# Attention of a cross-attention and expert layer: transposed projections of 512 columns, sums of squares by a matmul, scores on four 32-row tiles

## The reference

```python
q = layernorm(x) @ Wq.T                      # 32 heads of 16
k, v = context @ Wk.T, context @ Wv.T        # split from one concatenated kv
q, k = rmsnorm(q), rmsnorm(k)                # t * rsqrt(mean(t*t over 16) + 1e-6), each head by itself
scores = einsum('bhnd,bhmd->bhnm', q, k) * 16 ** -0.5
out = einsum('bhnm,bhmd->bhnd', softmax(scores), v)
x = x + out
```

## Time and profile before

| | before |
|---|---|
| median of 3 runs | 1083.45 us |
| the profiled execution: span from first to last instruction | 1096.4 us |
| first score matmul starts | 42.3 us |
| last score matmul starts | 532.3 us |
| first instruction of the second block's VectorE work | 538.80 us |
| TensorE busy in the span | 1011.1 us, 92% |
| VectorE, ScalarE, GpSimd busy | 726.6, 475.6 and 287.0 us |

### The profile page before, as it was taken

The page is one execution under the profiler, slowest core; times in us unless marked ns, Lnnn a source line. Parts: engine busy times, 40 slices in busy tenths (PEclk is TensorE's granted clock), DMA queues, the critical chain, the costliest instruction groups (busy, mean ns, idle before and its releaser), DMA issues.

```text
span 1096.4 us, 20598 instructions
## 1 busy us (share of the span) xinstructions
PE 1011.1 (92%) x7368; PEld 791.9 (72%) x7369; DVE 726.6 (66%) x1686; ACT 475.6 (43%) x670; POOL 287.0 (26%) x194
## 2 busy tenths in 40 slices
PE   3699999998999989999699999999999999999776
PEld 3555556565555665555299899999999899999666
DVE  6677876756676675765456887547474774765378
ACT  2256556545666446656723324233333342432111
POOL 3434444432343433432100010110101010101552
PEclk9899999999999999999879999999999999999889
DMA  9430000010000100000131015424242433332564
GB/s 321 159 116 2 1 1 2 20 59 3 1 1 30 49 3 1 21 20 1 49 136 67 20 32 187 158 69 171 70 174 75 179 120 121 139 90 77 163 193 144
DMA packets 32636, 88.90 MB, mean 81 GB/s; under 512 B 5040, under 2 KB 6576, under 8 KB 29104
## 3 DMA queue, kind: packets, MB, share of 16 engines
q1 hardware_dynamic: 25680, 65.34, 16.3%
q0 software_dynamic: 6880, 22.55, 6.9%
HBM read 65.33 MB, written 22.54 MB: 80 GB/s over the span
## 4 chain that ended last, share of the span: by engine, by line
PE 44%; DVE 4%; another core or an unknown queue 2%; issue 1%; ACT 1%; DVEq 0%; ACTq 0%
PE u_ps L958 14%; PE y_ps L958 13%; PE z_ps L958 13%; PE xt_ps L971 2%; DVE x_sb L1391 1%; PE z_ps L952 1%; DVE g_sb L1332 0%; PE xt_ps L984 0%; DVE u_lo L1320 0%; DVE stats L1174 0%; DVE x_sb L1351 0%; DVE g_hi L1335 0%; ACT u_hi L1093 0%; DVE hot_row L1285 0%
## 5 line engine op out<-in xcount | busy, mean ns | idle before, releaser
L454 ACT ACTIVATE probs<-scores 128x1024 f32<-128x1024 f32 x256 | 247.8, 1030 | 164.7 <-PE scores L332 164.7
L204 POOL TENSOR_TENSOR rsqrt<-mean_sq,power 128x16 f32<-128x16 f32 (+1 forms) x69 | 193.0, 2798 | 312.2 <-DVE mean_sq L556 277.3
L958 PE MATMUL z_ps<-u_hi,w_sb 128*128 128x256 f32 x896 | 167.9, 285 | 2.0 <-DVE u_lo L1320 1.6
L958 PE MATMUL u_ps<-x_hi,w_sb 128*128 128x256 f32 x896 | 165.1, 282 | 4.4 <-issue 2.3
L958 PE MATMUL y_ps<-w_sb,g_hi 128*128 128x512 f32 x448 | 143.9, 402 | 12.6 <-DVE g_lo L1337 8.4
L1093 ACT ACTIVATE u_hi<-u_ps,b_ug 128x256 fp32r<-128x256 f32 x112 | 47.1, 472 | 237.0 <-PE u_ps L958 233.0
L958 PEld LDWEIGHTS u_ps<-x_hi,w_sb 128*128 128x128 f32 x896 | 140.4, 190 | 7.2 <-issue 3.8
L958 PEld LDWEIGHTS z_ps<-u_hi,w_sb 128*128 128x128 f32 x896 | 141.0, 190 | 2.9 <-DVE u_lo L1320 2.0
L344 PE MATMUL o_ps<-probs,v_sb 128*32 128x512 f32 x1024 | 136.4, 604 | 0.5 <-ACT probs L454 0.3
L958 PE MATMUL z_ps<-u_lo,w_sb 128*128 128x256 f32 x448 | 126.3, 282 | 0.1
L958 PE MATMUL u_ps<-x_lo,w_sb 128*128 128x256 f32 x448 | 125.9, 281 | 0.0
(11 more groups left out here) (149 smaller groups left out, 1774.4 us busy)
## 6 DMA issues: line engine op xcount, KB each, us to landing
w_raw<-w_all SPq DMA_DIRECT2D x27, 1024.0 KB, 6.9
y_dram<-y_sb SPq DMA_DIRECT2D x40, 256.0 KB, 2.1
ctx_sb<-ctx_t SPq DMA_DIRECT2D x4, 1024.0 KB, 7.3
out<-x_sb SPq DMA_DIRECT2D x16, 256.0 KB
y_dram<-zeros SPq DMA_DIRECT2D x1, 3584.0 KB, 23.6
x_sb<-x SPq DMA_DIRECT2D x1, 3072.0 KB, 20.1
xn_dram<-xn SPq DMA_DIRECT2D x12, 256.0 KB, 2.1
bd<-b_down SPq DMA_DIRECT2D x9, 256.0 KB, 3.4
```

Of the source, the lines that this page charges most:

```text
L204: nc.gpsimd.tensor_tensor(rsqrt[:, half, 0:width], mean_sq[:, half, 0:width], power[:, 0:width], ALU.pow).then_inc(rsqrt_ready, 1)
L454: nc.scalar.activation(probs[:, s % 2, 2 * a:2 * a + 2, :], scores[:, a], ACT.Exp, scale=float(HD) ** 0.5).then_inc(p_ready, 1)
L958: ins = nc.tensor.matmul(out_ps, stat[a], mov[b], start=(first and a + b == 0), stop=(last and a == 1), skip_group_check=True)
```

## The change

The attention's block is written anew, for all 16 units without a hardware loop. A unit is again a group of 8 heads with 8 steps.

- q and k are made **transposed**, head dimensions on partitions: 12 float32r matmuls of 512 columns each per group (`q_passes` in three parts of 4, `k_chunk` in four of 3). v is made for all 32 heads at a time, 12 matmuls per 128 context rows, 4 times per sequence (`v_all`). The normalized x has hi and lo now too.
- The **sums of squares** over 16 partitions come from ScalarE's square and one float32 matmul with a block matrix of ones (`sum_q`, `sum_k`). The inverse root is ScalarE's Ln and Exp and one Newton step, the latter on VectorE (`first_root_*`, `newton_*`).
- The **stack** of hi and lo is made by VectorE: a shuffle of the 32 lanes of each quadrant doubles 16 dimensions to 32, a cast makes hi, and one more instruction lo (`stack_q`, `stack_k`). A contraction is now over 32 rows, with k_hi and k_lo in two rounds: **8 score matmuls on four tiles of 32 rows**, into all four banks of `scores`.
- ScalarE takes **one exponential of 2048 columns** per step, and the next scores wait for it (`p_ready`, t).
- Two banks (`bank_a`, `bank_b`) take k, q and v, and one (`tr`) everything else.
- x, context and weights arrive in a layout that a DMA reads in one piece per partition; context and weights are loaded in another order, and the first expert's weights later.

The core of the diff, with functions that it calls:

```diff
@@ TensorE @@
-            def score(par, s):
-                g4, mt = divmod(s, MT)
-                for a in range(2):
...
-                        pe.wait_ge(p_ready, scr.now(2))
...
+            def scored(u, s):
+                t, (ab, mt) = STEPS * u + s, divmod(s, MT)
+                if mt == 0:
+                    pe.wait_ge(q_stacked, 2 * u + ab + 1)
+                    pe.wait_ge(k_stacked, 2 * u + ab + 1)
+                if t:
+                    pe.wait_ge(p_ready, t)
...
+                for part in (k_hi, k_lo):
+                    for j in range(QUADS):
+                        rows = slice(32 * j, 32 * j + 32)
+                        last = nc.tensor.matmul(scores[:, j, :], part[rows, u % 2, ab, mt * P:(mt + 1) * P],
+                                                q_st[rows, u % 2, ab, :], start=(part is k_hi), stop=(part is k_lo),
+                                                skip_group_check=True)
+                last.then_inc(sc_ready, 1)
+            def q_passes(u, part):
...
+                turns = [(c, a, b) for c in range(DC) for a, b in ((0, 0), (0, 1), (1, 0))]
+                for c, a, b in turns[4 * part:4 * part + 4]:
+                    last = nc.tensor.matmul(bank_b[:], (wq_hi, wq_lo)[a][:, g, c, :], (xt_hi, xt_lo)[b][:, c, :],
...
+            def k_chunk(u, c):
...
+                last = three(bank_a[:], (wk_hi[:, g, c, :], wk_lo[:, g, c, :]), (ctx_hi[:, c, :], ctx_lo[:, c, :]),
+                             c == 0, c == DC - 1)
+            def sum_q(u):
+                begin("tr", TR_AT, ("sum_q", u), tr_free)
+                pe.wait_ge(sqq_done, u + 1)
+                nc.tensor.matmul(tr[:], blocks[:], sq[:], start=True, stop=True).then_inc(tr_ready, 1)
+            def between(u, s):
...
+                if s == 0:
+                    if behind and g == 1:
+                        norm2_transposes(b - 1, 0)
+                    if more and g == 2:
+                        norm_transposes(b + 1, 2)
+                    if u + 1 < UNITS:
+                        k_chunk(u + 1, 2)
+                elif s == 1:
...
+                        k_chunk(u + 1, 3)
...
+                        out_transposes(u - 1, 1)
+                elif s == 2:
...
+                        sum_k(u + 1)
+                    if more and g >= 2:
+                        v_all(bank_b[:], b + 1, 2 * g - 4).then_inc(b_ready, 1)
...
+                elif s <= 5:
...
+                        q_passes(u + 2, s - 3)
+                    if s == 3 and behind and g == 1:
+                        gates(b - 1, 0)
...
+                    if s == 5:
+                        out_transposes(u, 0)
+                        if more and g >= 2:
+                            v_all(bank_a[:], b + 1, 2 * g - 3).then_inc(a_ready, 1)
...
+                elif s == 6:
...
+                        k_chunk(u + 2, 0)
...
+                else:
...
+                        sum_q(u + 2)
+                        k_chunk(u + 2, 1)
...
@@ ScalarE @@
-                        nc.scalar.activation(probs[:, s % 2, 2 * a:2 * a + 2, :], scores[:, a], ACT.Exp,
+            def log_q(u):
+                act.wait_ge(ssq_ready, u + 1)
...
+                nc.scalar.activation(r0[:], ssq[:], ACT.Ln).then_inc(act_step, 1)
...
+            for u in range(UNITS):
+                for s in range(STEPS):
+                    t = STEPS * u + s
+                    before_exp(u, s)
+                    act.wait_ge(sc_ready, t + 1)
...
+                    nc.scalar.activation(probs[:, t % 2], scores[:], ACT.Exp).then_inc(p_ready, 1)
@@ VectorE @@
+            def sums_q(u):
+                take_tr(("sum_q", u))
+                done(nc.vector.tensor_scalar(ssq[:], tr[:], HD * RMS_EPS, None, ALU.add))
+                dve.sem_inc(tr_free)
+                dve.sem_inc(ssq_ready)
+            def newton(at, sums):
+                done(nc.vector.tensor_tensor(r2[:], sums[:], r2[:], ALU.mult))
+                nc.vector.scalar_tensor_tensor(at[:], r2[:], -3.0, at[:], ALU.add, ALU.mult).then_inc(norm_done, 1)
+            def stack_k(u, ab):
...
+                done(nc.vector.stream_shuffle(twin[:], kn[:], (UPPER_TWICE, LOWER_TWICE)[ab]))
+                hi = k_hi[:, u % 2, ab, :]
+                done(nc.vector.tensor_scalar(hi, twin[:], sign[:, 0:1], None, ALU.mult))
+                nc.vector.scalar_tensor_tensor(k_lo[:, u % 2, ab, :], twin[:], sign[:, 0:1], hi.bitcast(FP32),
+                                               ALU.mult, ALU.subtract).then_inc(k_stacked, 1)
```

More of the change, by code:

```diff
@@ L174, in moe_layer @@
[L174 to L186 removed]
+        W_AT = {w: n for n, w in enumerate(("k0", "q0", "v", "q1", "k1", "q2", "k2", "q3", "k3"))}
@@ L417, in _ @@
[L417 to L431 removed]
+            used = {"a": 0, "b": 0, "tr": 0}
@@ new lines, in _ @@
+            high("v", wv_hi[:], v_raw[:], 0)
+            log_k(0)
+            root_k(0)
+            root2_k(0)
+            high("q1", wq_hi[:, 1], q_raw[:, 1], 1)
+            high("k1", wk_hi[:, 1], k_raw[:, 1], 1)
+            square_q(0)
+            for mt in range(2):
+                act.wait_ge(first_v, mt + 1)
+                nc.scalar.copy(v_sb[0][:, mt, :, 0:HD], scores[:, mt, :].rearrange("p (h d) -> p h d", d=HD))\
+                  .then_inc(v_ready, 1)
+            log_q(0)
@@ L715, in _, with take_tr @@
-            for k in range(3):
-                unit(k, 0, first=(k == 0), between=lambda s: behind(k, s))
-            assert seen[0] == TILES
-            def turn(r):
-                unit(3, r - 1)
-                for k in range(3):
-                    unit(k, r, ln2=r - 1)
-            loop_over_batches(dve, tallies, turn)
-            unit(3, BATCH - 1, last=True)
-            finalize(BATCH - 1, GROUPS - 1, 1)
+                dve.wait_ge(dve_step, steps[0])
+            def take_tr(use):
+                assert TR_AT[use] == taken[0], use
+                taken[0] += 1
+                dve.wait_ge(tr_ready, TR_AT[use] + 1)
@@ new lines, in _ @@
+            for i in range(BT):
+                xt_low(scores[:, i, :], i).then_inc(xt_split, 1)
+            sums_k(0)
+            weight_low("v", wv_lo[:], v_raw[:], wv_hi[:])
+            first_root_k(0)
+            newton_k(0)
+            stack_k(0, 0)
+            weight_low("q1", wq_lo[:, 1], q_raw[:, 1], wq_hi[:, 1])
+            weight_low("k1", wk_lo[:, 1], k_raw[:, 1], wk_hi[:, 1])
+            sums_q(0)
+            stack_k(0, 1)
+            first_root_q(0)
+            newton_q(0)
@@ L727, in moe_layer @@
+            stack_q(0, 0)
+            stack_q(0, 1)
+            for u in range(UNITS):
+                for s in range(STEPS):
+                    step(u, s)
+            finalize(UNITS - 1, 1)
         att.close()
```

1164 lines of the change are left out of this document (648 added, 516 removed).

## The result

The changed kernel takes 1066.11 us (median of 4, 1065.05 to 1072.24) beside 1083.78 us of the kernel before (4 runs, 1082.43 to 1084.23): a ratio of 0.9836, 95% interval 0.9809 to 0.9863, so a gain clear of the noise and below 2%. That is 17.7 us less, where 29.8 were forecast. The range of 1022 to 1082 held it; the size was too large by 12.

The account below looks back on a forecast made before the run. TensorE was taken as the bound. Start 43.6, units 430.0 and VectorE stalls 30.3 put the last exponential's end at 503.9 against 534.1: -30.2, scaled to -29.8, so 1054 us; range 1022 to 1082.

Parts of the forecast that it names:

- the ring: Each attention step: scores, exponential, then the next scores, which wait for that exponential; a floor of 2.76 us per step.
- The slower rival: Score matmuls: four row tiles run two by two, 0.43 us more per step, 1108 us; chance 0.12.
- steps 1, 2, 4 and 5: Steps within a unit's eight, counted from 0: forecast 3.06, 3.06, 2.76 and 3.26 us without extras.
- step 7: Last of a unit's eight steps, with a float32 sum and a k chunk on TensorE: 3.33 us before VectorE stalls.
- VectorE late at the unit's end: Next unit's first exponential waits for ScalarE's log_q, which waits for VectorE's sums_q behind the last stack; 30.3 us in all.
- g = 1: Units with three norm and a norm_low on VectorE: stalls forecast at 1.9 + 2 x 2.0 us.
- No stall: Attention: VectorE never delays the exponentials, leaving the ring and TensorE alone; 1024 us, chance 0.18.
- The half clock behind a stall: TensorE after idling in a stall: 2 us of lost clock each, seven stalls, +14 us, claimed only in a rival.
- stalls double: Attention: late exponentials also cost TensorE clock, +14 us, and the shuffle is dearer, +6; 1074 us, chance 0.20.
- The start: Preparation before the attention's first score matmul: forecast at 43.6 us against 42.3 before, either side 41 to 47.
- entering unit 0: VectorE's lateness before the first unit's exponentials: 2.5 us of the 30.3 us of stalls.
- The base: Profiled span 1096.4 us, 1.2% above the runs' median, so the saving of 30.2 was carried over proportionally as 29.8.

Follow-up runs that it names:

- an order that costs next to nothing: Changed kernel with a step's eight score matmuls issued in pairs of row tiles; 1081.28 us on a slower chip, ratio 0.9884.
- The moved statistics: Changed kernel with the next sequence's four-tile statistics moved from the last step of units 0, 3, 7 to the following unit's step 0; 1049.26 us, ratio 0.9693.
- the sums first: Changed kernel with VectorE's sums_q for the next q moved one step earlier, ahead of the unit's last stack and the statistics; 1041.41 us, ratio 0.9614.
- One moved line: Changed kernel with unit 0's sum_q on TensorE behind the first v tile instead of the fourth; 1059.86 us, ratio 0.9775.

## Why the prediction came out as it did

- **The bound and the ring: right.** 2.72 for 2.76 in steps without extras. The slower rival, 1108 us, is out by its price: 0.79 from scores to exponential, not 1.2, and an order that costs next to nothing. How the four tiles share the array is not shown. That a whole unit came out near was in part luck: in unit 12 steps 1, 2, 4 and 5 take 2.94, 2.72, 3.15 and 2.86, where 3.06, 3.06, 2.76 and 3.26 were forecast, and with 3.40 for step 7 the unit is 23.35 against 23.75.
- **VectorE late at the unit's end: right in mechanism and place.** Step 7 was forecast at 15 x 3.33 + 27.8 = 77.8 us and measured 83.6. The moved statistics confirm 3.9 us for each of three of its nine long waits. The 5.8 too little are mostly g = 1, units 1, 5, 9: 5.2 to 5.3 forecast, 6.4 measured; the 1.1 are the bank `tr`, which the same addition frees, and the transposes and the copy between it and the Ln (1.98 us instead of 0.87). The list of units in "what the profile would show" was carelessly drawn: in the changed kernel the Ln is late entering units 1, 2, 4, 5, 6, 8, 9, 10 and 13, not 12; the sum had used the right ones. "No stall" (1024) is out; with the sums first it comes within 17 us.
- **The half clock behind a stall: the mis-sized term.** I had it as a rival at 14 us and in the forecast at nothing. The stalls of units 0, 3 and 7 leave TensorE idle for 4.1 to 4.4 us and it then runs at 0.50. It is no fixed tail of a stall: behind waits of 2.6 us, after units 4, 8 and 12, the clock fell twice and once not (here after units 8 and 12):

```profile
327.50:330.00 2.50, 2.40 (x11) 1.66 (x15) 0.69 (x1) 2.33 (x2) 0.00 (x0) 0.50 0.00 0
448.20:450.00 1.80, 1.78 (x15) 1.01 (x15) 0.69 (x1) 1.71 (x2) 0.00 (x0) 1.00 0.00 0
```

  With the sums first, steps 0 and 1 of units 1, 4, 5, 8, 9 are 9.2 us shorter in sum (7.2 by the table, in which units 2, 6, 10 lose 2.1). That all of it is the clock is my reading of it. My argument against, that TensorE still has its chunk and the values' product in a stall, failed: both were done at 169.7 in the rows above. So the measured 1066 lies between the forecast and the rival "stalls double" (1074): that rival's mechanism is there, at 9 us instead of 14.
- **The start: mis-sized by 5.7.** I summed VectorE's and ScalarE's chain to the first scores, and left out what stands ahead of them in TensorE's own queue: q of unit 1, which waits for a bank that VectorE frees at the end of that chain. One moved line brings 43.4. No rival had this term.
- **Given back, 4.3:** entering unit 0, forecast at 2.5, cost 0.7 (the first exponential starts 1.52 behind its scores, where 0.78 is the ring's); all other steps together are 2.5 shorter than forecast. With start 5.7, step 7 5.8, clock 9.2, less 4.3, that is the 16.4 by which the last exponential ends later than forecast (520.3 against 503.9). The 2.5 are what is left over, not measured by themselves.
- **The base:** of that, 4 us did not show in the time, and that was luck. Between profiles without the first one's disturbance (1080.5 and 1064.1), the attention gives 14.3 us and the rest 2.1, for the runs' 17.7. I had supposed that the 13 us between the first span and the median spread over everything in proportion; they were in the second block alone.

## What to carry to other kernels

When a change takes an engine off the bound, walk the new bound's queues for the small instruction that another engine waits for, and see what stands ahead of it: here one move of a 0.7 us instruction was worth more (24.7 us) than the rewrite (17.7 us). Price a wait of TensorE of some 4 us with what its clock costs behind it, by rows of such a wait in the same trace. And ask of such an instruction whether it also frees something: here it freed a bank as well. And an engine that is busy for two thirds of a phase can still set the time, if it meets the others several times a unit: work moved out of one meeting's way can come late to the next.
